# Local attention: both banks of probabilities summed by DVE, none by ACT's accumulator

## What is computed

```
for i in range(DEPTH):                       # DEPTH = 6
    x = attn_layer(shift_tokens(x), Wqkv[i], q_scale[i], k_scale[i], Wo[i]) + x
    x = ffn_layer(shift_tokens(x), ln_g[i], ln_b[i], W1[i], b1[i], W2[i], b2[i]) + x

# attn_layer: q, k = l2norm(...) * scale, rotary tables, then
sim  = jnp.einsum('bhwie,bhwje->bhwij', bq, bk2) * QK_SCALE
sim  = jnp.where(mask, -jnp.finfo(sim.dtype).max, sim)
attn = jax.nn.softmax(sim, -1)
out  = jnp.einsum('bhwij,bhwje->bhwie', attn, bv2)
```

## Time and profile before

| | us |
|---|---|
| median of 3 runs | 3058.05 (3054.85 to 3058.92) |
| the profiled execution, its own time | 3054.89 |
| its span in the profile | 3053.1 |
| PE busy | 2715.1 (89%) |
| DVE busy | 2102.4 (69%) |
| ACT busy | 1914.1 (63%) |
| POOL busy | 1582.0 (52%) |

### The profile page before, as it was taken

One profiled execution on the slowest core, in us unless ns is written; L12 is line 12 of the kernel. 1 busy time (PEld: TensorE's weight loads), 2 busy tenths in 40 slices (PEclk: granted clock), 3 DMA queues, 4 the chain that ended last, 5 costly groups with the idle time before them and its releaser, 6 DMA issues. The chain is left out here.

```text
span 3053.1 us, 69434 instructions
## 1 busy us (share of the span) xinstructions
PE 2715.1 (89%) x27218; PEld 1734.3 (57%) x27218; DVE 2102.4 (69%) x4064; ACT 1914.1 (63%) x5192; POOL 1582.0 (52%) x1845
## 2 busy tenths in 40 slices
PE   5996999899989998899889988999789977986995
PEld 2553777477746775577557764777334434542552
DVE  3764898598948994899679866897455434745663
ACT  3444888488848885788668875887323343554343
POOL 0523887288818882788468854887043003300530
PEclk8898999999999999999999999999989997998797
DMA  2001000100010001000100010000100000000000
GB/s 99 2 2 45 19 17 18 42 18 19 18 41 17 19 17 36 23 19 17 39 21 17 19 41 17 19 17 16 36 1 2 1 0 1 2 1 0 2 2 14
DMA packets 35934, 57.89 MB, mean 19 GB/s; under 512 B 7200, under 2 KB 32800, under 8 KB 33952
## 3 DMA queue, kind: packets, MB, share of 16 engines
q1 hardware_dynamic: 35616, 53.52, 5.6%
HBM read 27.28 MB, written 1.05 MB: 9 GB/s over the span
## 5 line engine op out<-in xcount | busy, mean ns | idle before, releaser
L1052 POOL TENSOR_TENSOR l_qk<-l_ta,l_tb 128x256 f32<-128x256 f32 x768 | 540.1, 738 | 113.9 <-DVE l_tb L1106 113.7
L674 POOL TENSOR_SCALAR qmr<-q_all,cf 128x256 fp32r<-128x256 f32 x128 | 116.2, 927 | 711.9 <-SPq L475 378.1
L1068 POOL TENSOR_TENSOR l_qk<-l_qk,l_rn 128x512 f32<-128x512 f32 x384 | 392.8, 1044 | 133.5 <-DVE l_rn L1131 133.5
L706 DVE TENSOR_REDUCE mrow<-ring 128x2 f32<-128x512 f32 x512 | 324.4, 684 | 197.7 <-PE ring L522 185.4
L1059 POOL TENSOR_TENSOR l_pr<-l_pr,l_rs 128x512 f32<-128x512 f32 x384 | 392.7, 1047 | 42.5 <-DVE l_rs L1121 42.5
L973 ACT ACTIVATE l_pr<-st,l_mn 128x128 f32<-128x128 f32 x1152 | 355.0, 384 | 85.9 <-DVE l_mn L1094 85.9
L659 ACT ACTIVATE pt<-st 128x512 f32<-128x512 f32 x384 | 200.2, 600 | 289.2 <-PE st L557 289.2
L1110 DVE TENSOR_REDUCE l_n<-l_sq 128x8 f32<-128x512 f32 x384 | 250.1, 660 | 27.6 <-ACT l_sq L982 26.8
L547 PE MATMUL st<-qm,k_all 32*128 32x512 f32 x1024 | 223.0, 672 | 0.0
L835 PE MATMUL ring<-l_wa,l_xs 128*128 128x512 f32 x384 | 195.0, 631 | 27.5 <-DMA l_wa<-in_wa 13.0
L522 PE MATMUL ring<-ktr,qmr 32*128 32x256 f32 x1024 | 198.5, 396 | 14.4 <-POOL qmr L674 11.9
(11 more groups left out here) (238 smaller groups left out, 6365.9 us busy)
## 6 DMA issues: line engine op xcount, KB each, us to landing
l_vm<-l_v SPq DMA_DIRECT2D x192, 96.0 KB, 2.0
l_wa<-in_wa SPq DMA_DIRECT2D x7, 2048.0 KB, 9.4
l_vm<-l_v SPq DMA_DIRECT2D x192, 32.0 KB, 1.9
l_wf<-in_wf SPq DMA_DIRECT2D x6, 580.5 KB, 3.7
w<-in_w SPq DMA_DIRECT2D x1, 2752.0 KB, 15.6
cf<-in_cf SPq DMA_DIRECT2D x1, 1123.0 KB, 17.7
x<-in_xT SPq DMA_DIRECT2D x1, 1024.0 KB, 4.8
ctxT<-in_ctxT SPq DMA_DIRECT2D x1, 1024.0 KB, 8.1
```

The lines of the kernel that those rows point to most:

```text
L706: dve.tensor_reduce(mrow[b % 2][:, t, j, 2 * p:2 * p + 2], bank_of(f"R{r}").rearrange("p (h k) -> p h k", h=2), AX.X, ALU.max).then_inc(ri ...
L1052: ins = pool.tensor_tensor(halves[0][:, :, x], halves[1][:, :, x], halves[2][:, :, 1 - x], ALU.add)
L1068: pool.tensor_tensor(part, part, t.rn[:, :, 4 * x:4 * x + 4].unsqueeze(3).broadcast_to([P, 2, 4, LHD]), ALU.mult).then_inc(qk_normed, 1)
```

## The change

ACT's exponentials of bank 0 lose their `accum_out`, so that no exponential accumulates. `reciprocals` on DVE gets a loop over both banks: for each it waits for that bank's exponentials and reduces the bank's four blocks of 128 probabilities to four sums. The semaphore `sums_ready` now rises twice in a step, and the wait ahead of the reciprocal is counted accordingly. The lines after the edits move up by one or come back to where they were: L1094, L1105, L1106, L1110 and L1114 of before are L1093, L1104, L1105, L1109 and L1113 after, and L1118, L1121, L1127, L1129 and L1131 keep their numbers.

```
             for x in range(4):
                 c, tile = divmod(x, 2)
-                kw = {"accum_out": t.ps[:, u, hh, x:x + 1]} if hh == 0 else {}
                 ins = act.activation(t.pr[:, u, hh, c, tile, :],
                                      bank(g, f"R{hh}", k)[:, x * P:(x + 1) * P], ACT.Exp, scale=-1.0,
-                                     bias=t.mn[:, u, hh, x:x + 1], **kw)
+                                     bias=t.mn[:, u, hh, x:x + 1])
             ins.then_inc(exps_done, 1)
...
         def reciprocals(N, k):
-            dve.wait_ge(exps_done, 2 * N + 2)
-            dve.tensor_reduce(t.ps[:, k % 2, 1, :], t.pr[:, k % 2, 1, :, :, :].rearrange("p c t q -> p (c t) q"),
-                              AX.X, ALU.add).then_inc(sums_ready, 1)
-            dve.wait_ge(sums_ready, N + 1)
+            for hh in range(2):
+                dve.wait_ge(exps_done, 2 * N + hh + 1)
+                dve.tensor_reduce(t.ps[:, k % 2, hh, :], t.pr[:, k % 2, hh, :, :, :].rearrange("p c t q -> p (c t) q"),
+                                  AX.X, ALU.add).then_inc(sums_ready, 1)
+            dve.wait_ge(sums_ready, 2 * N + 2)
             dve.reciprocal(t.rs[:, k % 2, :, :], t.ps[:, k % 2, :, :]).then_inc(recip_ready, 1)
```

## The result

| | before | after |
|---|---|---|
| median of 6 runs each, us | 3056.67 (3054.41 to 3059.99) | 3108.74 (3105.13 to 3122.06) |
| profiled span, us | 3053.1 | 3103.3 |
| PE / DVE busy, us | 2715.1 / 2102.4 | 2731.8 / 2207.6 |
| ACT / POOL busy, us | 1914.1 / 1582.0 | 1846.6 / 1582.4 |

The changed kernel takes 1.0174 times as long, with a 95% interval from 1.0154 to 1.0194: 52 us slower. ACT has 768 instructions fewer and 68 us less to do, DVE has 192 reductions and 105 us more.

A forecast was written before the change was run, and what follows sets the result against it. It took a loop over POOL's pair of L1059, which holds two small DVE instructions, as the bound. Profiled 3054.9 + 98 for lost floors - 7 at the depth ends = 3146, so 3149 us as median; range 3032 to 3163, its own 3125 to 3165.

The forecast's parts named there:

- the loop over POOL: Inner steps: L1127 is released when POOL's pair of L1059 ends, which sets the step, 7.87 us when plain.
- Where the floor comes to stand: DVE's floor L1114 moves to 321.45, 0.03 to 0.05 us before the recorded start of POOL's second L1059.
- The bracket from the earlier trace: At POOL's pair: the takeover by its second L1059 lies between 0.105 and 0.02 us before that instruction's recorded start.
- I take that it loses: At POOL's second L1059: the floor misses its turn and ends behind it, at 322.55, delaying everything after; chance 0.42.
- the copy at 0.02: Trace row cited for losing: DVE copy L1088, issued 0.02 us before POOL's second L1059, lasted 1.20.
- Rival B: At POOL's pair: some floors win, as POOL's starts shift by 0.02 us; at half, 3094 us; chance 0.15.
- rival A: At POOL's pair: the floor still wins, plain steps 0.12 us shorter, 19 us won in all, 3039 us; chance 0.33.
- rival C: On DVE: stalls belong to the small instructions, its chain is serial, about +0.34 us per step, 3110 us; chance 0.10.
- The price of a loss: Inner steps: a lost floor adds 0.65 us (plain), 0.80 (addition to y), 0.16 (copy); 98 us over six depths.
- The ends of the depths: Last two steps and about once at the start of each depth: ACT's 0.39 us is saved, 7 us in all.
- PE's wait for the copy of k: On PE: its waits of 0.2 to 0.4 us for ACT's copy of k (L992) go away.
- The accumulator reads: On ACT: four reads per step cost 0.39 us (1.39 against 1.00), 75 us of ACT's time over 192 steps.

The follow-up runs named there:

- e2: Kernel before without its floor (the DVE maximum with 1e-24 on the squared norms); ACT waits for the sums of squares instead: 3032.61 us.
- e1: Kernel before with ACT's half alone: no exponential accumulates, DVE sums only bank 1, the sums of bank 0 are left out: 3028.19 us.
- e3: Changed kernel plus a DVE memset of 64 unused columns ahead of the sums of squares, so the floor is issued later: 3141.0 us.
- e4: Changed kernel with the reduction of bank 0 over 96 of 128 columns, so the floor is issued earlier: 3030.64 us.
- e10: Changed kernel with the reduction of bank 0 over 120 of 128 columns, so the floor is issued earlier: 3032.56 us.
- e11: Changed kernel with the reduction of bank 0 over 124 of 128 columns, so the floor is issued earlier: 3038.94 us.
- e6: Changed kernel with the floor computed by a tensor_reduce with max over pairs with 1e-24 instead of a tensor_scalar: 3018.26 us.
- e5: Kernel before with DVE's half alone: all accumulation kept, DVE also sums bank 0 into a tile nobody reads: 3121.12 us.
- e8: Kernel before with the floor computed by a tensor_reduce with max instead of a tensor_scalar: 3030.62 us.

## Why the prediction was right, and where it was not

**The bound.** The reading of the loop over POOL held: e2 and e1 moved DVE's work by 0.3 to 0.4 us and the held instruction absorbed it, ending 0.03 to 0.04 behind POOL each time. No run took POOL's pair away; that it is the holder rests on these ends, on the edge at its second instruction (e3, e4, e10, e11) and on e6.

**Where the floor comes to stand.** I had it issued 0.03 to 0.05 before the second's recorded start; its median lead in the changed kernel is 0.055. The bracket from the earlier trace rows, 0.105 to 0.02, was right as well: counted over the changed kernel, e3, e5, e10 and e11, every lead above 0.080 won and every one below 0.031 lost.

**"I take that it loses".** This is the step that failed, in part. I let every floor lose, on the grounds that back-to-back instructions leave POOL no idle time and that the nearest row, the copy at 0.02, lost. 68% lost. The copy of the earlier trace rows is no exception (the 42 first copies beside a pair in the kernel before were issued within 0.019 of the second's start, before or behind it, and all took 1.20), but it came 0.03 later than the floor, and at this edge 0.03 is much of the difference: 0.06 later all are lost, 0.025 earlier none (e3, e10). And the scatter was taken too small. Rival B had 0.02 for it; the leads in the changed kernel go from 0.083 to 0.018, three times that and most of the bracket, so that a floor put at the bracket's middle could well fall on both sides. By B's own formula with the share that the trace shows, 3058 + 0.68 x 91 - 0.32 x 19 = 3114, against 3109 measured; the forecast's 3149 is 40 us too high. The sign held, since by those prices the kernel is slower as soon as more than 19 in 110 floors lose.

**What was luck.** The measured 3109 lies in the range of 3032 to 3163 because that range reached from rival A to the forecast. The forecast's own range, 3125 to 3165, missed it by 16 us, and what happened was rival B, at a chance of 0.15. The figure nearest to the measured one is rival C's 3110, whose mechanism the experiments refuted: the total alone would have pointed to the wrong cause.

**The price of a loss.** +0.65, +0.80 and +0.16 were forecast; all-lost steps in e3 are 0.67, 0.81 and 0.17 longer. The sum, 98 us, was 100.

**Rival A's price.** A winning plain step was put at 0.12 less and took 0.13 less. Its total was too small, though, by what lies outside the inner steps: 19 us, where the kernels in which no floor loses gained 25 to 36 (e1, e4, e6, e10).

**The ends of the depths.** I put 7 us on them from ACT's shorter exponentials. The last step went from 6.89 to 6.52, nearly as sized, in all six depths of e1 (2 us) and in three of the changed kernel; in its other three it grew to between 7.48 and 7.78, which stays open. What lies outside the inner steps (the last steps among it) fell by 13 in the changed kernel and by 18 in e1; but it also fell by 11 and 17 in e2 and e8, which keep every accumulation. So most of it isn't the accumulator's, and how much is stays open.

**The waits of ACT and PE.** I said that PE's wait for the copy of k goes. It did not: 48.9 us against 46.8. In e1 it fell by half to 22.0, so ACT's half removes half of it, and lost floors bring it back: counted from the records of the changed kernel, the wait is 0.34 us in a step that follows a lost floor and 0.17 in one that follows a won one (0.34 in every step of e3, 0.13 in e1). By the code this is POOL's late L1067 handed on, as PE's turn of q and k waits for it and ACT's copy of k for that turn. POOL's idle time of over 1 us before L1067 came as said. The accumulator reads were put at 0.39 us in four; the first bank's exponentials went from 1.39 to 1.02 from start to start, so they cost 0.37.

**Rival C** fell with e2 (no change in a plain step) and e3 (32 us for 0.06), though its 3110 was close.

## What to carry to other kernels

Where a tiny DVE instruction lasts longer than its shortest record and ends just behind one of POOL's, ask not how much work an edit adds to DVE but on which side of POOL's next instruction the tiny one comes to stand. Within 0.1 us of that edge expect a mixture, price both sides, and time several launches. The cure is another form of the tiny instruction (a reduction for a tensor_scalar) or another place: here the changed kernel went from a loss of 1.7% to a gain of 1.3%, and of 1.5% with the copy moved too. The other form alone, without the change, gave 0.7% (e8).

## What the runs showed of the hardware

- Handover between two back-to-back POOL instructions: a DVE tensor_scalar gets in or waits a whole POOL instruction, nothing between, and the recorded starts don't tell which. In the changed kernel winners were issued 0.083 to 0.031 us before the second's recorded start, losers 0.077 to 0.018, medians 0.056 and 0.054. (In e11 a loser was 0.080 ahead.) By the Trainium skill (the section cited above) the one that issues first has the ports; 123 floors with the earlier recorded start lost, so here the recorded starts don't order the two to within 0.08 us.
- The first L1058 lets go before its recorded end. Floors issued 0.13 before that end (e10) took 0.175, as if free; those issued 0.23 before it (e4) took 0.26, 0.09 more than their own 0.17, which puts the release at about 0.14 before the end (an estimate from these two).
- The stretch between two depths, from the last minima of one to the first of the next, takes between 67 and 74 us in every kernel, and the longer ones mostly have the lower granted clock. Two of the five such stretches in the kernel before, and two in e1_act_only (columns as in the earlier trace rows):

```profile
859.99:931.57 71.58, 61.15 (x242) 28.81 (x240) 39.78 (x77) 32.40 (x68) 18.08 (x24) 0.92 0.14 46
...
1180.56:1252.15 71.59, 59.48 (x241) 27.86 (x240) 39.98 (x77) 32.58 (x68) 18.09 (x24) 0.94 0.15 46
```

```profile
850.50:917.56 67.06, 55.66 (x221) 25.45 (x222) 39.65 (x77) 31.35 (x60) 18.07 (x24) 0.97 0.15 49
...
1792.77:1859.83 67.06, 55.66 (x221) 25.50 (x222) 39.53 (x77) 31.20 (x59) 18.08 (x24) 0.97 0.15 49
```

  The five together are 352.8 us before, 339.9 in e1 and 348.6 in e2. That is 13 of the 30 us that e1 gained, in a part of the program that the edit hardly touches. What shifts the clock there was not tried.
